# Four transformer layers on one core: biases, quantized weights and layer 3's attention weights requested in an earlier stage, and layer 3's context values computed one batch at a time

## The reference, cut to what matters

```python
x = x + tanh(g_xattn[l]) * attention_l(layernorm(x), ctx, ...)   # l = 0..3
x = x + tanh(g_ffn[l])   * ffn_l(layernorm(x), ...)

# layers 0 and 2: 16 heads of 8, with biases; layer 2 with a mask
q = x @ Wq + bq;  k = y @ Wk + bk;  v = y @ Wv + bv

# ffn of layer 2: weights are int32 (384 x 128, 384 x 128, 128 x 384)
w = w_int * (1 / 127)
h = silu(x @ w_gate.T) * (x @ w_up.T);  out = h @ w_down.T

# attention of layer 3: 8 heads of 64, no biases inside
q = x @ Wq;  k = ctx @ Wk;  v = ctx @ Wv          # each W is 128 x 512
attn = softmax(q @ k.T / 8);  out = (attn @ v) @ Wo + bo
```

## Time and profile before

| what | value |
|---|---|
| three runs | 1097.50, 1100.67 (median), 1102.53 us |
| the profiled execution: its time | 1095.08 us |
| the profiled execution: its span | 1093.3 us |
| mean granted TensorE clock | 0.913 of full speed |
| busy: PE, DVE, ACT, POOL | 879.5, 746.9, 565.1, 414.0 us |
| setup, until layer 0's attention starts | 16.68 us |
| layer 2's attention starts | 702.27 us |
| layer 2's feed-forward starts | 813.53 us |
| layer 3's attention starts | 873.81 us |

### The profile page before, as it was taken

One profiled execution on the slowest core, in us unless ns is written; L12 is line 12 of the kernel. 1 busy time (PEld: TensorE's weight loads), 2 busy tenths in 40 slices (PEclk: granted clock), 3 DMA queues, 4 the chain that ended last, 5 costly groups with the idle time before them and its releaser, 6 DMA issues. The chain is left out here.

```text
span 1093.3 us, 17068 instructions
## 1 busy us (share of the span) xinstructions
PE 879.5 (80%) x5336; PEld 666.8 (61%) x5336; DVE 746.9 (68%) x1844; ACT 565.1 (52%) x1091; POOL 414.0 (38%) x559
## 2 busy tenths in 40 slices
PE   1899585789999994888888888489966668995795
PEld 0677463666666653666666666368854437995573
DVE  3699577589999984666757656468856514555786
ACT  1587263367777772545646454257743333432364
POOL 1543214133344431565656656444311042321143
PEclk9899688679999996999999999789988889998699
DMA  4000000000000001000000000000000020000001
GB/s 129 9 2 2 1 0 24 1 21 21 22 22 21 22 21 39 1 1 1 1 1 1 1 1 1 2 2 2 2 22 1 0 77 1 1 2 1 0 1 39
DMA packets 25926, 14.13 MB, mean 13 GB/s; under 512 B 11095, under 2 KB 25326, under 8 KB 25710
## 3 DMA queue, kind: packets, MB, share of 16 engines
q1 hardware_dynamic: 25838, 13.04, 4.4%
HBM read 11.99 MB, written 1.05 MB: 12 GB/s over the span
## 5 line engine op out<-in xcount | busy, mean ns | idle before, releaser
L1495 POOL TENSOR_TENSOR L1f_h<-L1f_h,L1f_gb 128x512 f32<-128x512 f32 (+1 forms) x96 | 152.2, 1588 | 104.6 <-DVE L1f_h L1788 96.2
L762 ACT ACTIVATE L_pt<-bank 128x512 f32<-128x512 f32 x224 | 127.0, 597 | 40.7 <-PE bank L637 26.6
L423 POOL TENSOR_TENSOR L_kc<-L_kc_all,const 128x256 fp32r<-128x256 f32 x96 | 58.8, 616 | 154.7 <-PE bank L637 73.6
L1624 ACT ACTIVATE L1f_a<-bank 128x512 f32<-128x512 f32 (+1 forms) x96 | 57.3, 596 | 111.8 <-PE bank L1549 111.8
L1788 DVE TENSOR_TENSOR L1f_h<-L1f_a,bank 128x512 f32<-128x512 f32 (+1 forms) x96 | 65.5, 682 | 70.2 <-ACT L1f_a L1624 69.6
L1796 DVE TENSOR_TENSOR L1f_h_lo<-L1f_h,L1f_h_hi 128x512 fp32r<-128x512 f32 (+1 forms) x96 | 88.0, 917 | 11.1 <-ACT L1f_h_hi L1637 11.1
L892 DVE TENSOR_REDUCE L_ms<-bank 128x2 f32<-128x512 f32 x128 | 83.6, 684 | 4.1 <-PE bank L595 3.5
L749 ACT ACTIVATE L_part<-bank,L_bias_ca,const 128x256 fp32r<-128x256 f32 x128 | 68.7, 562 | 29.5 <-PE bank L572 28.5
L1547 PE MATMUL bank<-L1f_xt_hi,big_hi 128*128 128x512 f32 (+1 forms) x192 | 77.5, 403 | 0.1
L1549 PE MATMUL bank<-L1f_xt_hi,big_lo 128*128 128x512 f32 (+1 forms) x192 | 76.5, 398 | 0.0
L1548 PE MATMUL bank<-L1f_xt_lo,big_hi 128*128 128x512 f32 (+1 forms) x192 | 76.3, 397 | 0.0
(11 more groups left out here) (410 smaller groups left out, 2505.0 us busy)
## 6 DMA issues: line engine op xcount, KB each, us to landing
L_raw<-in_L_ffn_w_dram SPq DMA_DIRECT2D x8, 176.0 KB, 2.3
L_raw<-in_L_ffn_v_dram SPq DMA_DIRECT2D x8, 176.0 KB, 2.5
const<-in_const_dram SPq DMA_DIRECT2D x1, 1036.0 KB
x<-in_x_dram SPq DMA_DIRECT2D x2, 512.0 KB
L_raw<-in_L_ffn_w_dram SPq DMA_DIRECT2D x8, 128.0 KB, 2.6
mask<-in_mask_Bx1xSxS_ff_dram SPq DMA_DIRECT2D x2, 512.0 KB
out_dram<-x SPq DMA_DIRECT2D x2, 512.0 KB
L_raw<-in_L_ffn_w_dram SPq DMA_DIRECT2D x8, 48.0 KB, 2.4
```

The lines of the kernel that those rows point to most:

```text
L762: act.activation(pt[:, g // 2, (g % 2) * NS + (HEADS_1[i] if own_keys else i)], b_st[(g * NS + i) % 2][:], ACT.Exp, scale=scale).then_inc( ...
L1495: pool.tensor_tensor(h[0:m, r], h[0:m, r], gb[0:m, gate_slot(c)], ALU.mult).then_inc(sem["h_done"], 1)
```

## The change

Four things change. The eight `bias_t` loads of layer 0 are issued in `setup` ahead of the `w_att` pieces, and the eight of layer 2 in `setup` behind them and ahead of SP's waits; `bias_t` becomes a buffer of the program, one for each layer. `wi` and the five loads of layer 3's attention are issued by SP in layer 2's attention, behind its `bo` load. In layer 2's feed-forward the three `big_lo` subtractions stand behind the first `scale` on DVE, and PE waits for them at its first projection instead of before its first transposes. In layer 3's attention the eight value products leave the opening; a step `context_values` makes one batch's product per pass, in `b_turn`, with a copy on ACT and a wait on POOL ahead of `values`; `y` waits for the copy.

```diff
@@ Program.__init__
+        self.bias_t = {layer: sb(f"bias_t{layer}", [2 * NG, P], F32) for layer in (0, 2)}
+        self.bias_in = {layer: self.sem(f"bias_in{layer}") for layer in (0, 2)}
+        self.wi_in, self.w3_in = self.sem("wi_in"), self.sem("w3_in")
@@ setup, sync
+                def load_bias(layer):
+                    names = {0: ("L0_xattn_bq", "L0_xattn_bkv"), 2: ("L2_xattn_bq", "L2_xattn_bk")}[layer]
+                    for i, name in enumerate(names):
+                        for t in range(4):
+                            sp.dma_start(pr.bias_t[layer][NG * i:NG * i + NG].rearrange("g (h t d) -> g h t d", h=GH, t=4)[:, :, t],
+                                         ins[name][0:D].rearrange("(g h d) -> g h d", g=NG, h=GH)).then_inc(pr.bias_in[layer], 16)
+
+                load_bias(0)
                 for dst, src in (
...
                     sp.dma_start(dst, src).then_inc(w_in, 16)
+                load_bias(2)
                 sp.wait_ge(x_in, 32)
                 sp.wait_ge(w_in, 11 * 16)
@@ STEPS_3
-    ("values", 1), ("proj", 1, 1), ("pv", 0, 0), ("sums", 0), ("scores", 1, 0), ("scores", 1, 1), ("parts", 0), ("y", -1), ("keys", 2, 0),
+    ("context_values", 1), ("values", 1), ("proj", 1, 1), ("pv", 0, 0), ("sums", 0), ("scores", 1, 0), ("scores", 1, 1), ("parts", 0), ("y", -1), ("keys", 2, 0),
@@ attention, sync
-                    for i, (name, row) in enumerate({0: (("L0_xattn_bq", 0), ("L0_xattn_bkv", 0)), 2: (("L2_xattn_bq", 0), ("L2_xattn_bk", 0))}[layer]):
-                        for t in range(4):
-                            sp.dma_start(bias_t[NG * i:NG * i + NG].rearrange("g (h t d) -> g h t d", h=GH, t=4)[:, :, t],
-                                         ins[name][0:D].rearrange("(g h d) -> g h d", g=NG, h=GH)).then_inc(sem["bias_dma"], 16)
...
                 sp.dma_start(bo[:], ins[{0: "L0_xattn_bo", 1: "L1_xattn_bp", 2: "L2_xattn_bo"}[layer]].partition_broadcast(P)).then_inc(sem["bo_in"], 16)
+                if layer == 2:
+                    for dst, src in ((pr.wi[:, 0:3], ins["L2_ffn_w_gate"].rearrange("(c p) d -> p c d", p=P)),
+                                     (pr.wi[:, 3:6], ins["L2_ffn_w_up"].rearrange("(c p) d -> p c d", p=P)),
+                                     (pr.wi[:, 6:9], ins["L2_ffn_w_down"].rearrange("d (c p) -> d c p", p=P))):
+                        sp.dma_start(dst, src).then_inc(pr.wi_in, 16)
+                    for dst, src in ((pr.w3[:, 1], ins["L3_xattn_Wk"]), (pr.w3[:, 0], ins["L3_xattn_Wq"]), (pr.w3[:, 2], ins["L3_xattn_Wv"]),
+                                     (pr.w3[:, 3].rearrange("p (c n) -> p c n", n=D), ins["L3_xattn_Wo"].rearrange("(c p) n -> p c n", p=P)),
+                                     (pr.bo3[:], ins["L3_xattn_bo"].partition_broadcast(P))):
+                        sp.dma_start(dst, src).then_inc(pr.w3_in, 16)
@@ attention, tensor, p_bias
-                        pe.wait_ge(sem["bias_dma"], 16 * 8)
+                        pe.wait_ge(pr.bias_in[layer], 16 * 8)
@@ attention3, tensor
-                pe.wait_ge(sem["loaded"], 80)
+                pe.wait_ge(pr.w3_in, 80)
...
-                for e in range(B):
-                    bank = pr.bank[(NC + e) % 8]
-                    if e >= 4:
-                        pe.wait_ge(sem["prep_act"], e - 4 + 1)
-                    pe.matmul(bank[:], pr.ctx_t2[:, e].rearrange("p a s -> p (a s)"), wv[:], start=True, stop=True).then_inc(sem["prep_pe"], 1)
-                pe.wait_ge(sem["prep_act"], 12)
+                pe.wait_ge(sem["prep_act"], 4)
...
+                def context_values(b):
+                    pe.wait_ge(sem["xt_lo"], b + 1)
+                    pe.matmul(b_turn[:], pr.ctx_t2[:, b].rearrange("p a s -> p (a s)"), wv[:], start=True, stop=True).then_inc(sem["v_done"], 1)
@@ attention3, tensor, y (likewise for the last two batches)
-                        pe.wait_ge(sem["xt_lo"], b + 3)
+                        pe.wait_ge(sem["v_taken"], b + 3)
@@ attention3, scalar
+                def context_values(b):
+                    act.wait_ge(sem["v_done"], b + 1)
+                    act.copy(v_all[:, b], b_turn[:]).then_inc(sem["v_taken"], 1)
@@ attention3, gpsimd, values
+                    pool.wait_ge(sem["v_taken"], b + 1)
@@ attention3, gpsimd (before the batches; the vector engine drops its wait for prep_act)
-                pool.wait_ge(sem["prep_act"], 12)
+                pool.wait_ge(sem["prep_act"], 4)
@@ ffn, layer 2, tensor
-                pe.wait_ge(sem["prep_dve"], PREP_DVE)
+                if layer != 2:
+                    pe.wait_ge(sem["prep_dve"], PREP_DVE)
...
+                    if layer == 2 and i == 0 and c == 0:
+                        pe.wait_ge(sem["prep_dve"], PREP_DVE)
@@ ffn, layer 2, vector (the same three subtractions, moved behind the first scale)
-                    dve.wait_ge(sem["loaded"], LOADED)
+                    dve.wait_ge(pr.wi_in, 48)
...
+                    if layer == 2 and i == 0:
+                        low_weights()
+
+                def low_weights():
+                    for m in range(3):
+                        cols = slice(m * 384, (m + 1) * 384)
+                        dve.wait_ge(sem["prep_act"], m + 1)
+                        prep(dve.tensor_tensor(lo[:, cols], pr.bank[m][:, 0:384], hi[:, cols].bitcast(F32), ALU.subtract))
```

53 lines of the change are left out of this document (19 added, 34 removed).

## The result

| kernel | median, us | range (runs) | ratio to the kernel before, 95% |
|---|---|---|---|
| before | 1100.87 | 1097.50 to 1102.53 (4) | |
| after | 1090.22 | 1085.16 to 1094.54 (4) | 0.9896 [0.9853, 0.9939] |
| after, measured once more | 1085.26 | 1080.82 to 1095.02 (4) | 0.9882 [0.9824, 0.9941] |

The change makes the kernel faster by 1.0%, and by 1.2% in the second measurement. 1085.4 was predicted, with a range of 1079 to 1092. The ratios are estimated from the single runs, leaving out those in a slower state that some executions of any program show, so they are not quite the quotients of the medians. The first median lies outside the forecast's own range of 1081 to 1089, next to the rival of 1090.5 (layer 3 opening at half clock); the second lies on the forecast. Neither says which mechanism is right, as the stages show.

The account below looks back on a forecast made before the run. TensorE was taken to bound layer 3's batches, and load waits the stage openings. 1.4 - 4.9 - 3.8 - 14.2 + 6.2 = -15.3 us, taken from the three-run median 1100.67, gave 1085.4; range 1079 to 1092, the forecast's own 1081 to 1089.

Parts of the forecast that it names:

- layer 3 opening at half clock: Rival: layer 3's first two windows run PE at half clock, up to 13 us, likely about 5; 1090.5 us; chance 0.15.
- setup and layer 0: SP's longer issue queue starts layer 0 7.1 us later, 5.7 given back: a loss of 1.4 us, bounds 0 and 7.1.
- layer 2's attention: Opening no longer waits for `bias_t`, so the turn of x comes earlier: a gain of 4.9 us, lower bound 3.4.
- layer 2's feed-forward: `wi` is there early, so the first projection comes at 821.5 instead of 825.34: a gain of 3.8 us, 2.6 to 4.3.
- layer 3: first turn: Layer 3's opening loses its load wait and value products; turn at 880.8 instead of 894.98: a gain of 14.2 us.
- layer 3: from the first turn on: Layer 3's batches: seven value products at 0.88 us in full passes, batch 0's free: a loss of 6.2 us, bounds 0 and 12.6.
- a delay of 2 us on POOL is covered: Layer 3's batch 0: POOL's `split` may come 2 us later, since POOL then waited 3.52 us before L1051; no cost.
- Products that stall: Rival: in layer 3's batches PE or ACT waits for the other each time, 12.6 us instead of 6.2; 1091.8 us; chance 0.09.
- Products hidden: Rival: layer 3's value products fall in idle time that PE's rows do not show; 1079.2 us; chance 0.06.
- A late setup not given back: Rival: setup's later end costs 7.1 us instead of 1.4; 1091.1 us; chance 0.07.
- Loads hidden anyway: Rival: something else at the openings was as late as the loads, so their waits save nothing; about 1100 us; chance 0.05.
- Clock lost in the batches: Slower case: gaps in layer 3's passes drop the clock, up to 11.57 us more per batch; three give 1120 us; chance 0.04.

Follow-up runs that it names:

- short_setup: The changed kernel with layer 2's biases issued in layer 1's attention and eight `w_att` pieces of layers 1 and 2 in layer 0's attention; 1084.06 us, ratio to before 0.9839.
- chopped: The changed kernel with POOL's subtraction of layer 3's next weights cut into eight instructions; 1080.41 us, ratio to before 0.9823.
- values_first: The changed kernel with layer 3's value products, copies and waits back in the opening, loads still early; 1089.85 us, ratio to before 0.9904.
- chop_early: chopped with batch 0's value product moved behind the key products, batches 1 and 2 behind the first scores, 3 behind the second; 1086.29 us, ratio to before 0.9864.
- again: The changed kernel, unaltered, profiled and timed once more; 1085.26 us, ratio to before 0.9882.
- filler: chop_early with one more 128 x 512 matmul behind the first split, its result unread; 1088.67 us, ratio to before 0.9894.

## Why the prediction came out as it did

The time was inside the range and the signs of all steps were right. The sum was too good by 4.3 (11.0 measured of 15.3) in the first profile and by 2.65 in the second. So that the second measurement lay on 1085.4 was luck: the stages that the change touches had not saved that much. Term by term, the last column against the second profile of before:

| term | forecast | after | after, once more | after, against before once more |
|---|---|---|---|---|
| setup and layer 0 | +1.4 | +2.9 | +2.2 | +2.8 |
| layer 2's attention | -4.9 | -3.2 | -4.7 | -3.2 |
| layer 2's feed-forward | -3.8 | -4.9 | -4.6 | -3.8 |
| layer 3: first turn | -14.2 | -14.1 | -14.1 | -13.0 |
| layer 3: from the first turn on | +6.2 | +8.3 | +8.6 | +6.0 |
| sum | -15.3 | -11.0 | -12.6 | -11.2 |

The two profiles of before agree in the sum and differ by up to 2.3 us in single terms, so a term's distance from its forecast is known no better than that.

**Setup and layer 0.** The queue came as worked out (SP done at 22.99 against 23.05, whose four parts as printed add up to 23.03), but the stage began 1.2 behind it, not 0.72, so it started at 24.19 instead of 23.8. The successor of L516 came 1.45 after that, as forecast (1.4): 25.64 against 23.77 before, a loss of 1.9 where 1.4 stood. The rest, up to 2.9 in the first profile and 2.2 in the second, lies in the length of layer 0's attention, which varied from 96.5 to 98.6 us over kernels with the same code there; I have not settled it. short_setup shows that the queue's part can be avoided.

**Layer 2's attention.** The turn of x came 5.66 after the start, forecast 5.7, before 10.58. The mask is what PE waits for now, as the prediction named it, and it costs nothing. The eight loads behind `bo` (1.6 MB) did not show as a wait in this opening. The stage is shorter by 3.2 in one profile (mean granted clock 0.91) and 4.7 in the other (0.93), again with the same code.

**Layer 2's feed-forward.** The first projection came at 7.77, forecast 8.0, before 11.77. The subtractions behind the scaling ended 5.71 after the start, forecast 5.8.

**Layer 3's opening.** Forecast 7 us from the start to the first turn, measured 7.01. That the numbers meet is luck, for the path was another. The prediction had the key products end last, with `scale` already done. In after `scale` was not done: it waited 3.29 us for POOL's last memset, which ended 6.15 after the start (rstd took 3.34 instead of 2.91), and ran its 0.65 only then. The prediction gave POOL as the lower bound, without `scale` behind it. The key products took 5.10 instead of 6.15, at a clock of 0.72 instead of 0.60, and that was worth nothing. Moving POOL's clearing ahead of its rstd brought the turn to 6.46.

**Layer 3's batches: the step that was mis-sized.** The price of a product in a full pass was right: 12.42 against 11.57, 0.85 where 0.88 stood. What failed is the sentence that a delay of 2 us on POOL is covered because POOL waits 3.52 us before L1051. I asked who waits for POOL, and nobody does by a semaphore. But DVE's copy ran into POOL's subtraction. In before the subtraction began 4.47 us behind the turn and they overlapped only in its last 1.2 us; in after `values` had waited 1.89 us for ACT's copy, the subtraction began 6.86 behind the turn, and DVE's copy, at 7.5 as before, met 3.6 us of it. The term read 7 x 0.88 = 6.2; five full passes cost 4.25, the tail behind the last turn 0.5, the first two passes 2.6 and 0.9. In chopped, with the blockade reduced to one piece, the same term is 3.5: the first two passes are then 0.5 and 0.75 shorter than in before. So two errors of the term partly cancel: what it named cost 3.5 and not 6.2, since the first two passes, with a product more each, came out shorter than in before, at full clock; and what it left out cost 4.8 (122.92 less 118.16), the clock behind the blocked copy included. Against the second profile of before, whose first two passes were slowed by the clock, the same term reads 6.0 and would have looked right. The row that should have warned me was in the trace of before: a copy of 32 elements in 1.23 us beside seven of 0.18.

**The rivals.** Layer 3 opening at half clock: not in after at the place I named, since batch 0's product stood there, though the prediction counted on that product only as free work; behind the blocked copy the clock did fall, at a price of about 1.7 (14.93 against 13.25 in chopped). In four kernels without the product it fell at the first scores, values_first among them, which has all eight value products ahead of its first turn. I had held these to be what kept the clock up; the one product behind the first split did more for it. Products that stall: excluded, PE shows no wait for the values' copy and the passes are 12.42. Products hidden: excluded. A late setup not given back: of 7.5 and 7.6 us, 4.6 and 5.4 came back. Loads hidden anyway: excluded in three openings, whose waits are gone. Clock lost in the batches: excluded, 1.00 in the window of a regular pass.

**The move of the values** was the part of the change with the least behind it: I counted it within two terms, -7.7 in the opening and +6.2 behind it. By values_first its net is 0 as the change has it, and by chopped it is a gain of 5.1 once the copy is not blocked.

## What to carry to other kernels

Requesting a load a stage earlier is worth what ended last behind it, and nothing is requested for free: each issue costs the queue that makes it 0.47 us or more, and a stage whose end is that queue gets longer. When an instruction moves on one engine, look at what will run beside it and not only at who waits for it: an unusually long row of a trivial instruction (here 1.23 us beside 0.18) is a place that a small shift makes expensive. Compare stages when a program has stretches whose clock varies from run to run, and before taking work out of a thin stretch of TensorE, measure whether that work was keeping the clock.

## What the runs showed of the hardware that was not expected

- A copy of 128 x 32 floats on DVE took 0.18 us alone and up to 3.61 us beside a subtraction of 128 x 1920 on POOL (4.22 us), ending 0.05 us behind it; with the subtraction in eight pieces of 0.66 us it took 0.72. A reduction from PSUM on DVE beside the same subtraction took its usual 0.69.
- With one 128 x 512 product more, its result unused, layer 3's attention took 117.11 us instead of 119.17: the granted clock stayed at 1.00 instead of 0.50, and sixteen small matmuls took 2.05 us instead of 3.79. The Trainium skill, TensorE: Matmul & The Clock Gate, section HAM oscillation — how this bites in real kernels, tells of matmul bursts that start throttled again after a long wait. The window of after behind the wait of 4.43 us agrees (granted clock 0.50); the fall in chop_early came in a stretch whose longest wait was 1.05 us, which that section doesn't describe.
- The same 1712 matmuls of layer 1's attention took PE 206 to 225 us (206.29 in again, 224.75 in filler) from one execution to another, at mean clocks of 0.91 to 0.83, although PE was busy for more than 80% of that stage each time.
- A DMA issue on SP came every 0.47 us for a piece of `w_att`, and four of the bias loads, 16 runs of 8 floats each, took 2.61 to 2.84 us.
